# Token attention on one Trainium2 core: where the next input's moments are taken, and which engine normalises it

## The chip, the cores and the metric

The kernel runs on one core of a Trainium2 chip. The metric is the device time of one execution in microseconds (us), given as the median of several runs. The engines are TensorE (PE, with its weight loads shown apart as PEld), VectorE (DVE), ScalarE (ACT), GpSimd (POOL) and SyncE (SP).

## What is computed

The kernel is a stack of four residual blocks, each `x = x + layernorm(f(layernorm(x)))`. The change touches the first one alone, the token attention, on an input of 32 sequences of 256 tokens by 128 features:

```python
def _layernorm(x, axis=-1, eps=1e-05):
    m = jnp.mean(x, axis=axis, keepdims=True)
    v = jnp.var(x, axis=axis, keepdims=True)
    return (x - m) / jnp.sqrt(v + eps)

x = x + _layernorm(_L0_attn_ref(_layernorm(x, axis=-1), ...), axis=-1)
```

`_L0_attn_ref` has 16 heads of 8 features. Its scores are `alpha * tanh(q k / beta)` plus two bilinear terms in tanh bits of the input; then come a causal mask, a softmax over 256 tokens, the values and an output projection.

## The kernel before, in words

**Pipeline.** `token_attention` (from line 482 on) takes one sequence of 256 tokens, two tiles of 128, through four stages. In each step of the pipeline four sequences are in flight: `ahead` (its input is normalised and transposed), `front` (q, k, v and the bilinear left side are projected), `back` (scores, softmax, the first half of the values) and `done` (the rest: last transposes, division, output projection, the norm of the output and the residual). 32 sequences take 35 steps; 30 steps have both `ahead` and `back`, steps 2 to 31.

**Turns.** A step has six turns, 0 to 5. Each turn handles two of the twelve score units (128 x 512) of `back`, the "twins": PE computes raw and bilinear scores (L848, L854) and adds the mask (L858); ACT takes the tanh (L787); DVE sums (L672) and takes the negated row maximum (L682); POOL adds it (L613); ACT takes the exponential one turn later (`EXP = 1`, L804); PE transposes two turns later (`LAG = 2`, L868), and ACT (L748) and DVE (L710) copy the transposes out of PSUM. Every engine runs its own fixed program, in order; semaphores order the engines against each other. PSUM is used as two rings of four banks, one drained by ACT and one by DVE, so PE must wait for an older drain before it fills a bank: the second bilinear unit of a turn needs the bank of an earlier sum.

**What is placed where.** The constants at the head say which turn has which small job: k of `front` is projected in turn 1 and copied by ACT in four activations (L765); `DIVIDE = 3` is the division by the softmax sum (L691, L693 on DVE); `BACK = 4` is the transpose of the result (PE L948, ACT copy `oT` by L748), the output projection (PE L958) and its copy `y` (DVE L726); `OUT = 5` has the moments of `y` on DVE and, on POOL, `yvar` and `yrstd` ahead of the addition of turn 5 and `token_residual` behind it (L456, L459 and L462: subtract the mean, multiply by the inverse deviation, add to x).

**The input's norm, before.** `MOMENTS, SCALE = 1, 3`. At the end of turn 1, behind both maxima, DVE takes the moments of the next input's two tiles (two of L194, a small wait-separating copy at L150, two of L197). At the head of turn 2, ahead of that turn's addition, POOL computes `var` (L183), `rstd` (L187, a power) and `center = -mean * rstd` (L599, L603). At the end of turn 3 ACT computes `xn` with two activations, `Identity` with scale `rstd` and bias `center` (L811). PE transposes `xn` in turn 4 (L900).

The order of one turn on POOL, which matters most here, is:

```python
for i in range(turns):
    if ahead and i == MOMENTS + 1:
        norm.rsqrt(pool, "", ahead)
    ...
    for name in twins(i) if back else []:
        ...  # L613, the addition of the negated maximum
    if done and i == OUT and not done.last:
        token_residual(nc, pool, entry, done)
```

Of the kernel before, what the change touches and what calls it, by code (L numbers as in the profile page):

```python
# [10 lines left out]
ACT = mybir.ActivationFunctionType  # L11
ALU = mybir.AluOpType
AX = mybir.AxisListType

P = 128
# [466 lines left out]
def token_attention(nc, n_seq, x, w, c, behind, entry, following):  # L482
# [10 lines left out]

    VALUES, LATE_VALUES = {5: "yT0"}, {2: "yT1"}
    DIVIDE, BACK, OUT = 3, 4, 5
    MOMENTS, SCALE = 1, 3
    ahead_at = {4: ["xnT"], 5: ["right"]}
    front_at = {0: ["left", "q"], 1: ["k"], DIVIDE: ["v0", "v1"]}

# [28 lines left out]
    with ExitStack() as ctx:  # L528
        def sb(name, shape, dt=F32):
            return ctx.enter_context(nc.sbuf_tensor("t_" + name, shape, dt))  # L530

        def sem(name):
            return ctx.enter_context(nc.semaphore("t_" + name))
# [13 lines left out]
        inv_den = sb("inv_den", [P, TILES * TH])  # L547
        o = sb("o", [P, TILES, D])
        oT = sb("oT", [P, T])
        center = sb("center", [P, TILES])  # L550
        zero = sb("zero", [P, TILES])
        act_banks = [ctx.enter_context(nc.psum_tensor(f"t_act{i}", [P, BANK], F32)) for i in range(RING)]
        dve_banks = [ctx.enter_context(nc.psum_tensor(f"t_dve{i}", [P, BANK], F32)) for i in range(RING)]

# [12 lines left out]
        exped = Count(sem("exped"), in_turns(EXP), [], units[:2 * (turns - EXP)], late(EXP))  # L567
        den = Count(sem("den"), ["o"], [], [], ["o"])
        y, norm, vec, rst, updated = entry.y, entry.norm, entry.vec, entry.rst, entry.updated
        centred = Count(sem("centred"), ["minus", "center"], ["minus", "center"])  # L570
        scaled = Count(sem("scaled"), ["xn0", "xn1"], ["xn0", "xn1"])
        setup_pool, setup_act, setup_dve, setup_pe = (sem("setup_" + e) for e in ("pool", "act", "dve", "pe"))

        lam, scl = w["scalars"][:, 0:1], w["scalars"][:, 1:2]
# [7 lines left out]
        with nc.Block() as block:  # L582
            @block.gpsimd
            def _(pool):
                nc.gpsimd.memset(bilinear[:, :, :, :, :], 0.0).then_inc(setup_pool, 1)


                for u in range(2):
                    nc.gpsimd.memset(v[u][:, :, :, :], 0.0).then_inc(setup_pool, 1)
                nc.gpsimd.memset(zero[:, :], 0.0).then_inc(setup_pool, 1)  # L590
                pool.wait_ge(setup_pool, 4)
                for u in range(2):
                    nc.gpsimd.memset(v[u][:, :, :, TD:TD + 1], 1.0).then_inc(setup_pool, 1)

                def step(ahead, front, back, done):
                    for i in range(turns):
                        if ahead and i == MOMENTS + 1:
                            norm.rsqrt(pool, "", ahead)
                            nc.gpsimd.tensor_tensor(center[:, :], zero[:, :], norm.mv[""][:, :, 0], ALU.subtract)\  # L599
                                .then_inc(centred.sem, 1)  # L600
                            pool.wait_ge(rst.sem, rst.done("rstd", ahead))
                            pool.wait_ge(centred.sem, centred.done("minus", ahead))
                            nc.gpsimd.tensor_tensor(center[:, :], center[:, :], norm.rstd[""][:, :], ALU.mult)\  # L603
                                .then_inc(centred.sem, 1)
                        if done and i == OUT and not done.last:
                            norm.rsqrt(pool, "y", done)
                        for name in twins(i) if back else []:

                            n, gs, t = unit(name)
                            j = units.index(name)  # L610
                            pool.wait_ge(maxed.sem, maxed.done(name, back))
                            p = probs[:, j % SLOTS, :].rearrange("p (h j) -> p h j", h=len(gs))
                            nc.gpsimd.tensor_tensor(  # L613
                                p, p, neg_max[:, j, 0:len(gs)].unsqueeze(2)
                                .broadcast_to((P, len(gs), P * (t + 1))), ALU.add).then_inc(shifted.sem, 1)

                        if done and i == OUT and not done.last:
                            token_residual(nc, pool, entry, done)

                pipeline(pool, n_seq, step, 4, closing=lambda: following.open_pool(pool))  # L620
# [6 lines left out]
            def _(dve):  # L627
# [70 lines left out]
                def step(ahead, front, back, done):  # L698
                    for i in range(turns):
                        if done and i == OUT and not done.last:  # L700

                            wait_apart(nc, dve, c, to_dve.drained.sem, to_dve.drained.done("out", done))
                            norm.post_copied_moments(dve, done, y)
                        if back:
                            summed(i, back)
                        j, seq = lagging(i, LAG, turns, back, done)
                        if seq:
                            job = "pT" + twins(j)[1]
                            to_dve.wait_filled(dve, job, seq)
                            nc.vector.tensor_copy(pT[:, 2 * j + 1, :], to_dve.bank(job, seq)[:, :])\  # L710
                                .then_inc(to_dve.drained.sem, 1)
                        if back:
                            maxima(i, back)
                        if ahead and i == MOMENTS:
                            if not ahead.first:

                                dve.wait_ge(scaled.sem, scaled.done("xn1", ahead.before()))
                            norm.pre_moments(dve, ahead, x)
                        if done and i == DIVIDE:
                            divide(done)  # L720
                        if done and i == BACK:
                            if not done.first:

                                dve.wait_ge(updated.sem, updated.done("x", done.before()))
                            to_dve.wait_filled(dve, "out", done)
                            nc.vector.tensor_copy(y[:, :, :].rearrange("p a d -> p (a d)"),  # L726
                                                  to_dve.bank("out", done)[:, 0:T])\
                                .then_inc(to_dve.drained.sem, 1)
# [8 lines left out]
            def _(act):  # L737
# [39 lines left out]
                def step(ahead, front, back, done):  # L777
                    for i in range(turns):
# [26 lines left out]
                        for jobs, seq in ((ahead_at, ahead), (front_at, front)):  # L805
                            for job in jobs.get(i, []) if seq else []:
                                projected(job, seq)
                        if ahead and i == SCALE:
                            act.wait_ge(centred.sem, centred.done("center", ahead))
                            for t in range(TILES):  # L810
                                nc.scalar.activation(norm.xn[:, t], ahead.tile(x, t), ACT.Identity,  # L811
                                                     scale=norm.rstd[""][:, t:t + 1], bias=center[:, t:t + 1])\
                                    .then_inc(scaled.sem, 1)

                pipeline(act, n_seq, step, 4)

# [1 line left out]
            def _(pe):  # L818
# [7 lines left out]
                                           w["basis"][:, b, :], twT[:, :], start=True, stop=True)  # L826
                ins.then_inc(setup_pe, 1)
                pe.wait_ge(setup_dve, 11)
                pe.wait_ge(setup_pool, 6)

                def rows(n):

# [61 lines left out]
                def project(job, seq):  # L894
                    u, bank = seq.parity, to_act.bank(job, seq)
                    to_act.wait_free(pe, job, seq)
                    if job == "xnT":
                        for t in range(TILES):
                            pe.wait_ge(scaled.sem, scaled.done(f"xn{t}", seq))
                            ins = nc.tensor.transpose(bank[:, t * P:(t + 1) * P], norm.xn[:, t],  # L900
                                                      c["ident"][:, :])
                    elif job == "right":
                        to_act.wait_drained(pe, "xnT", seq)
                        ins = nc.tensor.matmul(bank[:, 0:T], w["bits"][:, :], xnT[u][:, :], start=True, stop=True)
                    elif job in ("q", "k"):
                        ins = nc.tensor.matmul(bank[:, 0:T], w["t" + job][:, :], xnT[u][:, :],
                                               start=True, stop=True)
                    elif job[0] == "v":
                        t = int(job[1])
                        ins = nc.tensor.matmul(bank[:, 0:D], xnT[u][:, t * P:(t + 1) * P], w["tv"][:, :],  # L910
                                               start=True, stop=True)
                    else:
                        to_act.wait_drained(pe, "right", seq)
                        for j in range(2):
                            ins = nc.tensor.matmul(bank[:, j * T:(j + 1) * T],
                                                   bilinear[:, j].rearrange("a n s b -> a (n s b)"),
                                                   bits[u][0:2 * BITS, 0, :], start=True, stop=True)
                    ins.then_inc(to_act.filled.sem, 1)
# [1634 lines left out]
```

## Time and profile before

| what | value |
|---|---|
| runs of the kernel before | 3971.15, 3981.91, 3981.96 us; median 3981.91 us |
| profiled execution | 3975.32 us, its span 3973.5 us |
| engines busy over the span | PE 95%, DVE 73%, ACT 67%, POOL 49% |
| granted TensorE clock, mean | 0.988 |
| token attention | from about 7 us to about 810 us of the span |

The span is what the profiler saw of the program; the execution's own time is 1.8 us longer. Times in timelines are microseconds from the span's start. "Busy" on PE is modelled from a pipeline and is not work at its peak. A bracket such as [0.88 <-PE ...] says how long the engine sat idle before the row and what the profile takes for the cause.

### The profile page before, as it was taken

The numbers are of one execution on the slowest core, as the hardware profiler recorded it, in microseconds if no ns is written. First come the engines' busy times: TensorE is split into PE (matmuls) and PEld (weight loads), VectorE is DVE, ScalarE is ACT, GpSimd is POOL, SyncE is SP. The second block draws the span as 40 slices with busy tenths as digits, with TensorE's granted clock in tenths as the row PEclk, the third lists the DMA queues.
The fourth block names the chain that finished last, engine by engine and source line by source line (L and its number), as shares of the span: only waits on it lengthen the run. The fifth ranks groups of instructions, "written<-read, shape, count | busy, mean of one in ns | idle before, by whom it ended". The sixth has DMA issues, their size and how long they took to land. (4 is left out here: it accounts for less than half of the span.)

```text
span 3973.5 us, 103557 instructions
## 1 busy us (share of the span) xinstructions
PE 3778.9 (95%) x34587; PEld 2912.5 (73%) x34841; DVE 2908.7 (73%) x6982; ACT 2654.1 (67%) x6409; POOL 1950.9 (49%) x1930
## 2 busy tenths in 40 slices
PE   7999999889999999999999999999999999999999
PEld 5767767657777765777776567777777777789998
DVE  6999999878888856888887855555655565656666
ACT  6999999868888833788886356666666666633333
POOL 4666666667777712667675433343334333411111
PEclk9999999989999989999999999999999999999999
DMA  3000000000000010000000100000000000000000
GB/s 107 1 0 0 0 0 0 1 22 21 20 24 20 20 28 20 14 16 13 16 13 19 31 26 1 0 0 0 0 0 0 0 0 0 0 7 9 9 9 9
DMA packets 69052, 47.64 MB, mean 12 GB/s; under 512 B 38361, under 2 KB 57953, under 8 KB 68833
## 3 DMA queue, kind: packets, MB, share of 16 engines
q1 hardware_dynamic: 68960, 46.43, 4.6%
q8 instruction: 56, 0.92, 0.1%
q14 instruction: 36, 0.29, 0.0%
HBM read 12.62 MB, written 4.19 MB: 4 GB/s over the span
## 5 line engine op out<-in xcount | busy, mean ns | idle before, releaser
L1871 ACT ACTIVATE l_probs<-l_act,l_neg_max 128x128 f32<-128x128 f32 (+1 forms) x1024 | 415.5, 425 | 274.0 <-DVE l_neg_max L1820 271.3
L1799 POOL TENSOR_TENSOR l_probs<-l_probs,l_sums 128x512 f32<-128x512 f32 x384 | 391.0, 1039 | 366.9 <-DVE l_sums L1828 366.9
L613 POOL TENSOR_TENSOR t_probs<-t_probs,t_neg_max 128x512 f32<-128x512 f32 x384 | 391.1, 1040 | 247.4 <-DVE t_neg_max L682 247.2
L1820 DVE TENSOR_REDUCE l_neg_max<-l_act 128x2 f32<-128x512 f32 (+1 forms) x384 | 247.0, 685 | 353.4 <-PE l_act L1983 160.7
L2197 ACT ACTIVATE e_hT<-e_act 128x512 f32<-128x512 f32 x256 | 152.7, 597 | 287.0 <-PE e_act L2218 287.0
L672 DVE SCALAR_TENSOR_TENSOR t_probs<-t_tanh_qk,scalars_sb,t_dve 128x512 f32<-128x512 f32 x384 | 269.7, 744 | 72.8 <-ACT t_tanh_qk L787 42.8
L1084 POOL TENSOR_TENSOR w_invQ<-w_lengthsQ,minus_half 128x16 f32<-128x16 f32 x64 | 243.8, 3810 | 87.8 <-DVE w_lengthsQ L1157 87.8
L2230 PEld LDWEIGHTS e_dve<-e_sb,e_hT 128*128 128x128 f32 x2048 | 269.6, 192 | 16.2 <-ACT e_hT L2197 3.0
L1071 POOL TENSOR_TENSOR w_swappedQ<-w_rawQ,w_table 128x512 f32<-128x512 f32 x128 | 162.1, 1288 | 242.9 <-ACT w_rawQ L1269 242.9
L2230 PE MATMUL e_dve<-e_sb,e_hT 128*128 128x128 f32 x2048 | 270.7, 275 | 2.6 <-ACT e_hT L2197 2.6
L2218 PE MATMUL e_act<-e_xnT,e_sb 128*128 128x256 f32 x1024 | 266.7, 383 | 0.0
L787 ACT ACTIVATE t_tanh_qk<-t_act,t_inv_beta 128x512 f32<-128x512 f32 x384 | 244.7, 697 | 29.3 <-PE t_act L848 29.1
L1376 PE MATMUL w_c<-wqkv_sb,w_hT 128*128 128x512 f32 x512 | 255.2, 622 | 6.0 <-ACT w_rawQ L1269 3.7
L848 PE MATMUL t_act<-t_k,t_q 32*128 32x256 f32 (+1 forms) x2048 | 221.1, 343 | 25.9 <-DVE t_probs L672 25.0
L1838 DVE COPY l_pT<-l_dve 128x512 f32<-128x512 f32 x384 | 242.8, 674 | 1.7 <-PE l_dve L1936 1.7
L682 DVE TENSOR_REDUCE t_neg_max<-t_probs 128x2 f32<-128x512 f32 (+1 forms) x384 | 243.9, 678 | 0.0
L1305 ACT ACTIVATE w_probs<-w_a,w_bias,w_invQ 128x128 f32<-128x128 f32 x512 | 185.5, 467 | 82.9 <-DVE w_bias L1186 82.9
L804 ACT ACTIVATE t_probs<-t_probs 128x512 f32<-128x512 f32 x384 | 230.4, 655 | 13.2 <-POOL t_probs L613 13.0
L1071 POOL TENSOR_TENSOR w_swappedK<-w_rawK,w_table 128x512 f32<-128x512 f32 x128 | 223.7, 1766 | 7.3 <-ACT w_rawK L1269 7.3
L1936 PE MATMUL l_dve<-ident_sb,l_probs 128*128 128x128 f32 x1536 | 208.7, 276 | 17.4 <-POOL l_probs L1799 11.9
L854 PE MATMUL t_dve<-t_bits,t_left 32*128 32x256 f32 (+1 forms) x2048 | 221.1, 343 | 0.0
L1921 PE MATMUL l_act<-l_kT,l_qT 64*128 64x128 f32 (+1 forms) x2048 | 219.6, 343 | 0.1
(257 smaller groups left out, 10283.5 us busy)
## 6 DMA issues: line engine op xcount, KB each, us to landing
w_v_mid<-w_v SPq DMA_DIRECT2D x128, 130.0 KB, 2.3
z<-w_z_copy SPq DMA_DIRECT2D x32, 128.0 KB, 2.0
h<-z SPq DMA_DIRECT2D x32, 128.0 KB
out<-x_sb SPq DMA_DIRECT2D x32, 128.0 KB, 1.8
h<-z SPq DMA_DIRECT2D x32, 127.0 KB
wqkv_sb<-L_ffn_wqkv SPq DMA_DIRECT2D x2, 768.0 KB, 6.7
kv_up_sb<-L_attn_w_kv_up SPq DMA_DIRECT2D x1, 1024.0 KB, 9.5
e_sb<-L_ffn_w SPq DMA_DIRECT2D x1, 1024.0 KB, 5.5
```

Of the source, the lines that this page charges most:

```text
L613: nc.gpsimd.tensor_tensor(p, p, neg_max[:, j, 0:len(gs)].unsqueeze(2) .broadcast_to((P, len(gs), P * (t + 1))), ALU.add).then_inc(shifted. ...
L672: nc.vector.scalar_tensor_tensor(probs[:, j % SLOTS, :], tanh_qk[:, j % TANHS, :], alpha, to_dve.bank("bil" + name, back)[:, :], ALU.mult, ...
L682: nc.vector.tensor_reduce(neg_max[:, j, 0:len(gs)], probs[:, j % SLOTS, :].rearrange("p (h j) -> p h j", h=len(gs)), AX.X, ALU.max, negate ...
L787: nc.scalar.activation(tanh_qk[:, j % TANHS, :], to_act.bank("raw" + name, back)[:, :], ACT.Tanh, scale=inv_beta[:, :])\
L1071: nc.gpsimd.tensor_tensor(swapped[kind][:, t, :].rearrange("p (h a d) -> p h a d", a=2, d=HD // 2), raw[kind][:, t, :].rearrange("p (h a d ...
L1084: nc.gpsimd.tensor_tensor(inv[kind][seq.parity][:, :], length[kind][:, :], c["minus_half"][:, 0:TILES * NH], ALU.pow).then_inc(gps.sem, 1)
L1376: ins = nc.tensor.matmul(of[kind].bank(kind, front)[:, t * BANK:(t + 1) * BANK], hT[:, t * P:(t + 1) * P], w["wqkv"][:, layer, at:at + INNER],
L1799: nc.gpsimd.tensor_tensor(p, p, sums[:, at, 0:len(hs)].unsqueeze(2) .broadcast_to((P, len(hs), P * (t + 1))), ALU.mult).then_inc(divided.s ...
L1820: nc.vector.tensor_reduce(neg_max[:, units.index(name), 0:len(hs)], to_act.bank("s" + name, back)[:, :].rearrange("p (h j) -> p h j", h=le ...
L1871: ins = nc.scalar.activation(probs[:, at % SLOTS, s * width:(s + 1) * width], bank[:, s * width:(s + 1) * width], ACT.Exp, bias=neg_max[:, ...
L2218: ins = nc.tensor.matmul(to_act.bank(f"h{e}", back)[:, f * T:(f + 1) * T], w["e1"][:, e, f * P:(f + 1) * P], xnT[back.parity][:, :], start ...
L2230: ins = nc.tensor.matmul(to_dve.bank(job, seq)[:, (e % half) * D:(e % half + 1) * D], hT[:, e % 2, f, t * P:(t + 1) * P], w["e2"][:, e, f, :],
```

## The change

The moments of the next input go from the end of turn 1 to the head of turn 0 on DVE. `var` and `rstd` go from the head of turn 2 to the head of turn 0 on POOL. `center`, with its constant `zero`, is gone. The two activations of ACT in turn 3 are gone: POOL computes `xn` behind its additions of turn 1, over both tiles at once, as a subtraction of the mean and a multiplication by `rstd`, both broadcast over the features. PE waits once for the product instead of once for each tile. The diff, without context that says nothing more:

```diff
-    MOMENTS, SCALE = 1, 3
+    MOMENTS, SCALE = 0, 1
...
-        centred = Count(sem("centred"), ["minus", "center"], ["minus", "center"])
-        scaled = Count(sem("scaled"), ["xn0", "xn1"], ["xn0", "xn1"])
+        scaled = Count(sem("scaled"), ["diff", "xn"], ["diff", "xn"])
...
+                def normalised(ahead):
+
+                    def each(a):
+                        return a.unsqueeze(2).broadcast_to((P, TILES, D))
+
+                    if not ahead.first:
+                        to_act.wait_filled(pool, "xnT", ahead.before())
+                    pool.wait_ge(rst.sem, rst.done("rstd", ahead))
+                    nc.gpsimd.tensor_tensor(norm.xn[:, :, :], ahead.tiles(x), each(norm.mv[""][:, :, 0]),
+                                            ALU.subtract).then_inc(scaled.sem, 1)
+                    pool.wait_ge(scaled.sem, scaled.done("diff", ahead))
+                    nc.gpsimd.tensor_tensor(norm.xn[:, :, :], norm.xn[:, :, :], each(norm.rstd[""][:, :]),
+                                            ALU.mult).then_inc(scaled.sem, 1)
...
                     for i in range(turns):
-                        if ahead and i == MOMENTS + 1:
+                        if ahead and i == MOMENTS:
                             norm.rsqrt(pool, "", ahead)
-                            nc.gpsimd.tensor_tensor(center[:, :], zero[:, :], norm.mv[""][:, :, 0], ALU.subtract)\
-                                .then_inc(centred.sem, 1)
-                            pool.wait_ge(rst.sem, rst.done("rstd", ahead))
-                            pool.wait_ge(centred.sem, centred.done("minus", ahead))
-                            nc.gpsimd.tensor_tensor(center[:, :], center[:, :], norm.rstd[""][:, :], ALU.mult)\
-                                .then_inc(centred.sem, 1)
...
+                        if ahead and i == SCALE:
+                            normalised(ahead)
...
+                        if ahead and i == MOMENTS:
+                            if not ahead.first:
+
+                                dve.wait_ge(scaled.sem, scaled.done("xn", ahead.before()))
+                            norm.pre_moments(dve, ahead, x)
                         if back:
                             summed(i, back)
...
-                        if ahead and i == MOMENTS:
-                            if not ahead.first:
-
-                                dve.wait_ge(scaled.sem, scaled.done("xn1", ahead.before()))
-                            norm.pre_moments(dve, ahead, x)
...
-                        if ahead and i == SCALE:
-                            act.wait_ge(centred.sem, centred.done("center", ahead))
-                            for t in range(TILES):
-                                nc.scalar.activation(norm.xn[:, t], ahead.tile(x, t), ACT.Identity,
-                                                     scale=norm.rstd[""][:, t:t + 1], bias=center[:, t:t + 1])\
-                                    .then_inc(scaled.sem, 1)
...
                     if job == "xnT":
+                        pe.wait_ge(scaled.sem, scaled.done("xn", seq))
                         for t in range(TILES):
-                            pe.wait_ge(scaled.sem, scaled.done(f"xn{t}", seq))
```

## Rows read from the trace of the kernel before

**Rows 1.** Busy time by stretch: us, then PE, PEld, DVE, ACT, POOL, clock, DMA.

```profile
100.00:700.00 600.00, 553.13 (x7733) 421.42 (x7782) 545.55 (x1106) 548.25 (x1159) 407.12 (x529) 1.00 0.00 0
```

**Rows 2.** Timeline of DVE: start, us of the group, engine, line, op, out<-in, count, [idle before].

```profile
410.40 1.27 DVE L682 TENSOR_REDUCE t_neg_max<-t_probs 128x4 f32<-128x512 f32 x2
412.55 1.41 DVE L672 SCALAR_TENSOR_TENSOR t_probs<-t_tanh_qk,scalars_sb,t_dve 128x512 f32<-128x512 f32 x2 [0.88 <-PE t_dve L868]
...
418.14 1.27 DVE L682 TENSOR_REDUCE t_neg_max<-t_probs 128x2 f32<-128x512 f32 x2
419.32 0.48 DVE L194 BATCH_NORM_STATS2 t_stats<-x_sb 128x6 f32 x2
...
420.35 1.41 DVE L672 SCALAR_TENSOR_TENSOR t_probs<-t_tanh_qk,scalars_sb,t_dve 128x512 f32<-128x512 f32 x2 [0.21 <-PE t_act L888]
...
426.94 0.42 DVE L693 TENSOR_TENSOR t_o<-t_dve,t_inv_den 128x256 f32<-128x256 f32 x1
427.61 1.41 DVE L672 SCALAR_TENSOR_TENSOR t_probs<-t_tanh_qk,scalars_sb,t_dve 128x512 f32<-128x512 f32 x2 [0.24 <-ACT t_tanh_qk L787]
```

**Rows 3.** Timeline of ACT in the same step, turns 1, 3 and 4.

```profile
416.94 1.17 ACT L804 ACTIVATE t_probs<-t_probs 128x512 f32<-128x512 f32 x2
417.99 1.57 ACT L765 ACTIVATE t_k<-t_act,places_sb 128x256 f32<-128x256 f32 x4
419.42 1.31 ACT L787 ACTIVATE t_tanh_qk<-t_act,t_inv_beta 128x512 f32<-128x512 f32 x2
...
425.10 0.63 ACT L804 ACTIVATE t_probs<-t_probs 128x512 f32<-128x512 f32 x1 [0.37 <-POOL t_probs L613]
425.63 0.41 ACT L771 COPY t_v<-t_act 128x128 f32<-128x128 f32 x2
425.94 0.88 ACT L811 ACTIVATE t_xn<-x_sb,t_center,t_rstd 128x128 f32 x2
426.72 1.26 ACT L787 ACTIVATE t_tanh_qk<-t_act,t_inv_beta 128x512 f32<-128x512 f32 x2
...
428.32 0.41 ACT L748 COPY t_oT<-t_act 128x256 f32<-128x256 f32 x1
```

**Rows 4.** Timeline of POOL: residual, addition of turn 0, norm, addition of turn 2.

```profile
413.15 0.61 POOL L456 TENSOR_TENSOR t_yn<-t_y,t_ymv 128x256 f32<-128x256 f32 x1
...
415.35 2.04 POOL L613 TENSOR_TENSOR t_probs<-t_probs,t_neg_max 128x512 f32<-128x512 f32 x2
...
420.89 0.20 POOL L183 TENSOR_TENSOR t_var<-t_mv,eps 128x2 f32<-128x2 f32 x1
421.16 0.71 POOL L187 TENSOR_TENSOR t_rstd<-t_var,minus_half 128x2 f32<-128x2 f32 x1
421.84 0.19 POOL L599 TENSOR_TENSOR t_center<-t_zero,t_mv 128x2 f32<-128x2 f32 x1
...
423.03 2.04 POOL L613 TENSOR_TENSOR t_probs<-t_probs,t_neg_max 128x512 f32<-128x512 f32 x2 [0.72 <-DVE t_neg_max L682]
```

**Rows 5.** Timeline of PE in the same step, turn 4.

```profile
425.67 0.38 PE L848 MATMUL t_act<-t_k,t_q 32*128 32x256 f32 x2
...
427.42 0.44 PE L948 MATMUL t_act<-ident_sb,t_o 128*128 128x128 f32 x2 [0.16 <-DVE t_o L693]
...
428.78 0.71 PE L958 MATMUL t_dve<-t_out_sb,t_oT 128*128 128x128 f32 x4 [0.70 <-ACT t_oT L748]
429.42 0.38 PE L848 MATMUL t_act<-t_k,t_q 32*128 32x128 f32 x2
```

**Rows 6.** Timeline of DVE in the next step: turn 5, and the moments again.

```profile
433.64 0.69 DVE L710 COPY t_pT<-t_dve 128x512 f32<-128x512 f32 x1 [0.21 <-PE t_dve L868]
...
443.17 0.48 DVE L194 BATCH_NORM_STATS2 t_stats<-x_sb 128x6 f32 x2
```

**Rows 7.** The residual's line 462: what its engine waited for (us, times).

```profile
  POOL t_yn L459: 6.0, 28
```

**Rows 8.** Timeline of PE near the start, the transpose of the second sequence.

```profile
25.50 0.77 PE L900 MATMUL t_act<-ident_sb,t_xn 128*128 128x128 f32 x2 [1.61 <-ACT t_xn L811]
```

More of the change, by code:

```diff
@@ L549, in token_attention @@
         oT = sb("oT", [P, T])
-        center = sb("center", [P, TILES])
-        zero = sb("zero", [P, TILES])
         act_banks = [ctx.enter_context(nc.psum_tensor(f"t_act{i}", [P, BANK], F32)) for i in range(RING)]
@@ L589, in _ @@
                     nc.gpsimd.memset(v[u][:, :, :, :], 0.0).then_inc(setup_pool, 1)
-                nc.gpsimd.memset(zero[:, :], 0.0).then_inc(setup_pool, 1)
-                pool.wait_ge(setup_pool, 4)
+                pool.wait_ge(setup_pool, 3)
                 for u in range(2):
                     nc.gpsimd.memset(v[u][:, :, :, TD:TD + 1], 1.0).then_inc(setup_pool, 1)
+                def normalised(ahead):
[9 more added lines that the diff above has]
+                                            ALU.mult).then_inc(scaled.sem, 1)
                 def step(ahead, front, back, done):
                     for i in range(turns):
-                        if ahead and i == MOMENTS + 1:
+                        if ahead and i == MOMENTS:
                             norm.rsqrt(pool, "", ahead)
-                            nc.gpsimd.tensor_tensor(center[:, :], zero[:, :], norm.mv[""][:, :, 0], ALU.subtract)\
-                                .then_inc(centred.sem, 1)
-                            pool.wait_ge(rst.sem, rst.done("rstd", ahead))
-                            pool.wait_ge(centred.sem, centred.done("minus", ahead))
-                            nc.gpsimd.tensor_tensor(center[:, :], center[:, :], norm.rstd[""][:, :], ALU.mult)\
-                                .then_inc(centred.sem, 1)
                         if done and i == OUT and not done.last:
@@ L828, in _ @@
                 pe.wait_ge(setup_dve, 11)
-                pe.wait_ge(setup_pool, 6)
+                pe.wait_ge(setup_pool, 5)
                 def rows(n):
```

## The prediction

> **What bounds the kernel now.** I read the busy time by stretch first. In the 600 us of steady token attention PE, DVE and ACT are each busy for 91 to 92 percent and POOL for 68 percent [rows 1]. No engine is the bound alone: the step is a ring of waits among three nearly full engines, and only a place on that ring is worth time. So I read the timeline of each engine over one step. The moments start at 419.32 in one step and at 443.17 in the next [rows 2, 6]: a step takes 23.85 us.
>
> The ring, followed through that step. Turn 1 of ACT is contiguous: exponentials 416.94, four copies of k 417.99, tanh of turn 2 at 419.42 [rows 3]. DVE's sum of turn 2 starts 0.93 us after that tanh, at 420.35; it follows the first of the two tanhs, although the row names an old PE event [rows 2]. So in turn 2 ACT is late, and not DVE. From 420.35 DVE then runs without a gap until the quotient at 426.94, waits 0.24 us for the tanh of turn 4, and sums at 427.61 [rows 2]. On PE the quotient's transpose starts at 427.42, 0.06 us behind DVE; the copy oT on ACT starts at 428.32, behind tanh and another copy; the projection follows at 428.78 and the scores of turn 5 at 429.42 [rows 3, 5]. From there PE is full to the transposes of turn 5, for which DVE's copy at 433.64 waits 0.21 us [rows 6]. POOL is beside the ring, with one tight place: three residual operations from 413.15, and without a gap the addition of turn 0 at 415.35 [rows 4]. Its second half ends at 417.39, and ACT's second exponential of turn 1 starts at about 416.94 + 0.53 = 417.47, with 0.53 taken from 425.10 to 425.63 [rows 3, 4]. The slack there is 0.05 us, given a hand-over of 0.03 us (POOL ends at 423.03 + 2.04 = 425.07, ACT starts at 425.10) [rows 3, 4].
>
> **The change part by part.**
>
> *Moments out of turn 1 on DVE.* They take 420.35 - 419.32 less the idle 0.21, which is 0.82 us [rows 2]. The gain is nothing: the sum of turn 2 waits for ACT's tanh anyhow, so the 0.82 us turn into idle time.
>
> *Moments into the head of turn 0 on DVE.* The cover is the idle 0.88 us before 412.55 [rows 2]. The maxima of turn 5 start at 410.40 and the next operation may start 1.18 us later (419.32 - 418.14 for the same pair), at 411.58; with 0.82 us of moments the sum may start at 412.40, before the 412.55 which ACT sets. Cost nothing, by 0.15 us. Were the cover gone, it would cost up to the whole 0.82 us a step. The new wait for `xn` of the sequence before is met since turn 1 of the step before.
>
> *`var` and `rstd` to the head of turn 0 on POOL.* Before, they stood between 420.89 and 421.84, and the addition of turn 2 was idle for 0.72 us behind them and `center` [rows 4]: free. Now they stand between the residual and the addition of turn 0, where POOL has no idle time. The price by start-to-start distances is 421.84 - 420.89 = 0.95 us [rows 4]. Queued behind them is the addition of turn 0, and ACT's exponential of turn 1 waits for that. The addition ends at 417.39 + 0.95 = 418.34, the second exponential starts at 418.37 in place of 417.47, k at 418.90 in place of 417.99, the tanh of turn 2 at 420.33, the sum of turn 2 at 421.26: +0.91 us (0.95 less the slack, with rounding). The scores of turn 3 follow the first half of that sum, since they need its bank, and DVE is contiguous to the quotient, so all of turns 2 and 3 are 0.91 us later. By spans the two operations would be 0.20 + 0.71 = 0.91 us [rows 4], and the delay 0.87 us.
>
> The rows thus give 0.95 by spacing and 0.91 by spans. The Trainium skill, Perfetto Trace Analysis, GPSIMD Engine Instruction, says that spans on this engine don't compose and that one should go by the distance between starts. By that rule the delay is 0.91 a step, otherwise 0.87; over 28 steps the two differ by about 1 us.
>
> *`center` gone from POOL.* The addition of turn 2 waits for DVE's maximum behind it [rows 4]. Nothing.
>
> *Two products on POOL behind the additions of turn 1.* Of the same shape as L456 [rows 4]: 0.61 us each, with the wait between them some 1.4 us, from 420.89 to about 422.3. The next addition waited for its maximum until 423.03 before, and will until about 423.94. Nothing; PE wants `xn` only in turn 4. The nearest bound from above: all of 1.4 us beyond the 422.23 at which `center` ended is still short of 423.03.
>
> *Two activations gone from ACT in turn 3.* 426.72 - 425.94 = 0.78 us of ACT's order [rows 3]. The tanh of turn 4 can then follow PE's raw scores instead. The last of these end at 425.67 + 0.38 = 426.05 [rows 5]; hand-overs in these rows take 0.03 to 0.06 us, and from PE to ACT I allow 0.11 (an estimate, the upper side), so 426.16 in place of 426.72. The sum of turn 4 can start only when the quotient is done, so DVE gains its idle 0.24 us [rows 2]. PE's path is tighter: the quotient's transpose ends at 427.42 + 0.44 = 427.86, so oT can be copied at 427.97 in place of 428.32 [rows 3, 5]. Gain 0.35 us at the projection and at the scores of turn 5. DVE's 0.24 is no closer limit, since its copy of turn 5 waits 0.21 for PE [rows 6]. What is late next is PE itself. From below the gain is 0.24, from above 0.56 (tanh alone); I take 0.35, the row of the wait that remains.
>
> **The sum.** Per step +0.91 - 0.35 = +0.56 us. The residual precedes turn 0 in 28 steps [rows 7], and all of these have `ahead`: 28 x 0.56 = 15.7 us. In steps 2 and 3 no residual stands ahead and only the gain is left, up to 2 x 0.35 = 0.7 us. At the start PE waits 1.61 us for the second sequence's `xn`, which ACT makes late, behind v [rows 8]; POOL will have it early, and the copy xnT can start when v is copied, about 1.3 us earlier. Together 15.7 - 0.7 - 1.3 = +13.7 us. On the profiled execution's 3975.3 us this is 3989.0 us. That execution is 6.6 us below the median of the runs, 3981.9 us; on the median it is 3995.6 us, +0.34 percent.
>
> **The rivals.**
>
> *POOL does not bite (other side).* The place is the second exponential of turn 1. If POOL's delay were under 0.05 us there, because the power runs while the residual is still being written, or because the residual ends sooner, then only the gain of turn 4 is left: 30 x 0.35 + 1.3 = 11.8 us faster, 3970.1 us on the median. For it: the moments are there by 412.4, 3 us before POOL needs them, and ACT loses 0.78 us of work. Against it: POOL works in order, and 415.35 has no idle time before it. It decides if the delay in turn 1 falls below 0.35 us.
>
> *POOL bites and turn 0 of DVE is not covered.* The margin of 0.15 us is small. If the moments end later than the tanh of turn 0 allows, the sums of turns 0 and 1 and with them PE's scores of turn 2 slip too. At worst 0.82 us more on the ring, 28 x 0.82 = 23 us, so 4018 us; with half of it 4007 us. For it: the tanh is only just later than DVE. Against it: the ring's delay lies behind turn 1, so turn 0 keeps its distances.
>
> *The delay is absorbed in part.* With the gain at its upper 0.56 and the delay at its lower 0.87 the step grows by 0.31 us: 28 x 0.31 - 2.0 = +6.7 us, 3988.6 us. This is the lower end of my own case, not a case apart.
>
> **How the numbers follow.** The forecast has 0.62, the first rival 0.23, the second 0.15. Under about 0.3 percent (12 us) a measurement of this kernel cannot tell from no change. My case runs from 3988 to 3999 us, around 3995.6; by the scatter of the runs, 11 us in three, it ends as slower with 0.45 and as same with 0.17. The first rival lies right on the limit of 0.3 percent: same 0.13, faster 0.10. The second: slower 0.13, same 0.02. That makes faster 0.10, same 0.32, slower 0.58. The range goes down to 3970, the first rival, and up to 4008, half of the second's extra cost.
>
> **What would show it right or wrong.** Right: a step of 24.4 us between two moments; on POOL `var` directly behind L462 and the addition directly behind `rstd`; a new idle time on ACT before its exponentials of turn 1, releaser POOL L613, about 0.4 us twice a step; DVE idle about 1.9 us before the sum of turn 2; that before the sum of turn 0 nearly gone; ACT's tanh of turn 4 waiting for PE. Wrong: a step of 23.5 us, with no wait of ACT on POOL in turn 1; or a step over 24.8 us with DVE contiguous through the head of turn 0.

## The result, and the profile after

The changed kernel takes 3984.87 us in the median of 22 runs, the kernel before 3974.2 us in the median of 22. The ratio is 1.0021, 95% interval [1.0012, 1.003]: slower, by about two thirds of the +0.34 percent that were forecast. The interval lies above 1, so 22 runs of each resolve a difference that the prediction held to be too small to tell from no change. The profiled execution's span is 3984.3 us, 10.8 us more than before; of these, 7.3 us are there by the end of the token attention. One run of a later kernel (norm at the head of turn 1) took 4014.07 us, with a mean granted clock of 0.942 where every other listed run has 0.986 to 0.993; no ratio below contains it.

The busy time of 100 to 700 us of the changed kernel, columns as in [rows 1]:

```profile
100.00:700.00 600.00, 544.99 (x7618) 413.44 (x7664) 533.41 (x1082) 529.36 (x1088) 419.85 (x518) 1.00 0.00 0
```

ACT fell from 548 to 529 us of 600, but PE and DVE fell too, by 8 and 12 us: in the same stretch fewer steps are done. Work was taken from ACT, and the ring became slower.

POOL's timeline of one step of the changed kernel, from the residual on, answers to [rows 4]:

```profile
415.85 0.73 POOL L462 TENSOR_TENSOR x_sb<-x_sb,t_yn 128x256 f32 x1 [0.21 <-POOL t_yn L459]
416.53 0.20 POOL L183 TENSOR_TENSOR t_var<-t_mv,eps 128x2 f32<-128x2 f32 x1
416.81 0.71 POOL L187 TENSOR_TENSOR t_rstd<-t_var,minus_half 128x2 f32<-128x2 f32 x1
417.49 2.04 POOL L617 TENSOR_TENSOR t_probs<-t_probs,t_neg_max 128x512 f32<-128x512 f32 x2
420.07 2.03 POOL L617 TENSOR_TENSOR t_probs<-t_probs,t_neg_max 128x512 f32<-128x512 f32 x2 [0.56 <-DVE t_neg_max L688]
422.07 0.61 POOL L599 TENSOR_TENSOR t_xn<-x_sb,t_mv 128x256 f32<-128x256 f32 x1
422.76 0.61 POOL L602 TENSOR_TENSOR t_xn<-t_xn,t_rstd 128x256 f32<-128x256 f32 x1
425.10 2.04 POOL L617 TENSOR_TENSOR t_probs<-t_probs,t_neg_max 128x512 f32<-128x512 f32 x2 [1.73 <-DVE t_neg_max L688]
```

The norm stands without a gap between the residual and the addition of turn 0, and holds that addition back by 417.49 - 416.53 = 0.96 us. The two products end at 423.4, and POOL then idles 1.73 us: they cost nothing.

ACT's timeline in the same step, turns 1, 3 and 4, answers to [rows 3]:

```profile
418.56 0.63 ACT L810 ACTIVATE t_probs<-t_probs 128x512 f32<-128x512 f32 x1 [0.31 <-POOL t_probs L617]
419.55 0.63 ACT L810 ACTIVATE t_probs<-t_probs 128x512 f32<-128x512 f32 x1 [0.37 <-POOL t_probs L617]
420.09 1.55 ACT L771 ACTIVATE t_k<-t_act,places_sb 128x256 f32<-128x256 f32 x4
421.52 1.28 ACT L793 ACTIVATE t_tanh_qk<-t_act,t_inv_beta 128x512 f32<-128x512 f32 x2
...
428.23 1.26 ACT L793 ACTIVATE t_tanh_qk<-t_act,t_inv_beta 128x512 f32<-128x512 f32 x2
429.38 0.59 ACT L754 COPY t_pT<-t_act 128x512 f32<-128x512 f32 x1
429.97 0.37 ACT L754 COPY t_oT<-t_act 128x256 f32<-128x256 f32 x1
```

Both exponentials of turn 1 now wait for POOL, and k and the tanh of turn 2 are late with them.

DVE's timeline, the answer to [rows 2]:

```profile
411.58 1.27 DVE L688 TENSOR_REDUCE t_neg_max<-t_probs 128x4 f32<-128x512 f32 x2
412.77 0.48 DVE L194 BATCH_NORM_STATS2 t_stats<-x_sb 128x6 f32 x2
...
413.35 0.24 DVE L197 BATCH_NORM_AGGREGATE t_mv<-t_stats 128x2 f32<-128x6 f32 x2
413.70 1.41 DVE L678 SCALAR_TENSOR_TENSOR t_probs<-t_tanh_qk,scalars_sb,t_dve 128x512 f32<-128x512 f32 x2
...
419.32 1.27 DVE L688 TENSOR_REDUCE t_neg_max<-t_probs 128x2 f32<-128x512 f32 x2
422.43 1.41 DVE L678 SCALAR_TENSOR_TENSOR t_probs<-t_tanh_qk,scalars_sb,t_dve 128x512 f32<-128x512 f32 x2 [1.84 <-PE t_act L868]
...
429.02 0.42 DVE L699 TENSOR_TENSOR t_o<-t_dve,t_inv_den 128x256 f32<-128x256 f32 x1
429.36 1.40 DVE L678 SCALAR_TENSOR_TENSOR t_probs<-t_tanh_qk,scalars_sb,t_dve 128x512 f32<-128x512 f32 x2
```

The moments fill the idle time ahead of the sum of turn 0, which starts 413.70 - 411.58 = 2.12 us after the maxima of turn 5; before it was 2.15 [rows 2]. From the maxima of turn 1 to the sum of turn 2 it is 422.43 - 419.32 = 3.11 us; before, 2.21. This is the loss: 0.90 us. The profile lays the 1.84 us of idle time to a PE event; the wait is for ACT's tanh, 421.52 + 0.91, as before the sum came at 419.42 + 0.93 [rows 2, 3]. In turn 4 the sum follows the quotient after 0.34 us, where it took 0.67: DVE waits for ACT no more.

PE's timeline at the end of turn 4, the answer to [rows 5]:

```profile
429.50 0.44 PE L948 MATMUL t_act<-ident_sb,t_o 128*128 128x128 f32 x2 [0.17 <-DVE t_o L699]
...
430.39 0.71 PE L958 MATMUL t_dve<-t_out_sb,t_oT 128*128 128x128 f32 x4 [0.24 <-ACT t_oT L754]
431.04 0.38 PE L848 MATMUL t_act<-t_k,t_q 32*128 32x128 f32 x2
```

The projection comes 0.89 us after the transpose of the quotient; before, 1.36 [rows 5]. This is the gain: 0.47 us in this step. The next `var` on POOL starts at 440.81, so the step is 440.81 - 416.53 = 24.28 us; before, 23.85 [rows 2, 6]. And 0.90 - 0.47 = 0.43.

### The profile page after: what moved, and what is told of

The parts are those of the page before. It is cut to its first block and busy times, and to the rows that moved or that the text cites. A ratio compares the mean times of both kernels' runs of the same rounds, so it can differ in the third digit from the quotient of the medians.

```text
span 3984.3 us, 103435 instructions
## 1 busy us (share of the span) xinstructions
PE 3780.9 (95%) x34587; PEld 2912.8 (73%) x34841; DVE 2906.3 (73%) x6982; ACT 2641.5 (66%) x6345; POOL 1977.2 (50%) x1929
## 5 line engine op out<-in xcount | busy, mean ns | idle before, releaser
L1936 PE MATMUL l_dve<-ident_sb,l_probs 128*128 128x128 f32 x1536 | 208.1, 275 | 17.8 <-POOL l_probs L1799 12.3
L854 PE MATMUL t_dve<-t_bits,t_left 32*128 32x256 f32 (+1 forms) x2048 | 220.2, 343 | 0.0
```

## The experiments

A step below is the distance between the moments of neighbouring sequences in the steady part; it varies by 0.03 us at most within a run. "Norm" stands for `var` and `rstd` on POOL. Ratios are those of the runs, not of the steps.

| kernel | step, us | ratio to before, 95% interval |
|---|---|---|
| before | 23.84 | |
| the change | 24.28 | 1.0021 [1.0012, 1.0030] |
| norm at the head of turn 1 | 23.39 | 0.9952 [0.9936, 0.9968] |
| products alone | 23.40 | 0.9949 [0.9930, 0.9968] |
| moments alone | 23.86 | 1.0002 [0.9993, 1.0011] |
| moments and norm in turn 0, ACT as before | 24.74 | 1.0060 [1.0045, 1.0076] |
| norm behind the addition of turn 0 | 23.39 | 0.9959 [0.9943, 0.9976] |
| a second power in turn 0 | 24.95 | 1.0075 [1.0054, 1.0096] |

**Norm at the head of turn 1.** The changed kernel, with `var` and `rstd` one turn later on POOL:

```diff
-                        if ahead and i == MOMENTS:
+                        if ahead and i == SCALE:
                             norm.rsqrt(pool, "", ahead)
```

> The changed kernel with var and rstd at the head of turn 1 on POOL, ahead of that turn's addition, in place of the head of turn 0. Theory (the power ahead of the addition of turn 0 is what costs): ACT's waits on POOL in turn 1 are gone, the 0.90 us between the sums of turns 1 and 2 go back to 4.1 us, only the gain of turn 4 (0.47 us, as the trace of the changed kernel has it) is left: a step of 23.4 us, about 17 us less than the kernel before (ratio 0.996). Rival (the two products on POOL, or POOL's load as such, cost): the step stays at 24.3 us and the time at that of the changed kernel, ratio 1.002.

It took 3958.68 us in the median of all its runs against 3977.36 us of the kernel before, where the expectation had 17 us less. POOL's timeline of this kernel, from the residual on:

```profile
405.96 0.73 POOL L462 TENSOR_TENSOR x_sb<-x_sb,t_yn 128x256 f32 x1 [0.21 <-POOL t_yn L459]
406.65 2.03 POOL L617 TENSOR_TENSOR t_probs<-t_probs,t_neg_max 128x512 f32<-128x512 f32 x2
408.65 0.19 POOL L183 TENSOR_TENSOR t_var<-t_mv,eps 128x2 f32<-128x2 f32 x1
408.92 0.71 POOL L187 TENSOR_TENSOR t_rstd<-t_var,minus_half 128x2 f32<-128x2 f32 x1
410.19 2.04 POOL L617 TENSOR_TENSOR t_probs<-t_probs,t_neg_max 128x512 f32<-128x512 f32 x2 [0.56 <-DVE t_neg_max L688]
```

The same two operations, one addition later, stand in a gap that ends with 0.56 us still idle. ACT's waits in that kernel, over 600 us of steady steps:

```profile
ACT t_probs L810 <- POOL t_probs L617: 9.5, 26, 0.4
```

Only the old wait of turn 3 is left, once a step; in the changed kernel the same row has 26.2 us in 75 waits, three a step. The place of `var` and `rstd` is what costs, and not the products or POOL's load, which is the same.

**Products alone.** The kernel before, with `center` and ACT's activations replaced by the two products, behind the additions of turn 2; moments and norm stay at their old places:

```diff
-    MOMENTS, SCALE = 1, 3
+    MOMENTS, SCALE = 1, 2
...
-                        if ahead and i == MOMENTS + 1:
+                        if ahead and i == SCALE:
                             norm.rsqrt(pool, "", ahead)
-                            nc.gpsimd.tensor_tensor(center[:, :], zero[:, :], norm.mv[""][:, :, 0], ALU.subtract)\
...
+                        if ahead and i == SCALE:
+                            normalised(ahead)
...
```

> The kernel before with one part of the change: moments stay at the end of turn 1, var and rstd at the head of turn 2, center and the two activations are gone and POOL takes the two products behind the additions of turn 2. Theory: this is the gain alone, 0.47 us a step, so a step of 23.4 us and about 14 us less than before (ratio 0.9965); POOL's addition of turn 3 may start 0.3 us late, which ACT doesn't feel. Rival (ACT's activations were covered, and what looks like a gain in turn 4 is given back by PE or DVE): step 23.85 us, ratio 1.000.

It took 3958.85 us against 3977.36 us: 18.5 us less, where 14 were expected. The profiles differ by 14.8 us at the end of the token attention (the next stage's first statistics, L322, start at 775.6 us in place of 790.4), so the expected size holds there; the rest of the difference is not explained by the steps. Here the products do delay the next addition, as POOL's timeline shows by the missing idle time behind them:

```profile
416.46 0.61 POOL L599 TENSOR_TENSOR t_xn<-x_sb,t_mv 128x256 f32<-128x256 f32 x1
417.15 0.61 POOL L602 TENSOR_TENSOR t_xn<-t_xn,t_rstd 128x256 f32<-128x256 f32 x1
417.72 2.04 POOL L617 TENSOR_TENSOR t_probs<-t_probs,t_neg_max 128x512 f32<-128x512 f32 x2
```

The additions of turn 3 start 3.26 us after those of turn 2 (414.46), where it was 3.10 in the other kernels. The step is the same to 0.01 us: the exponentials of that turn come late enough. So the relief of ACT alone is worth 0.44 us a step. That `center` is gone from POOL as well is no rival: the addition of turn 2 behind it was idle for 0.72 us even with it [rows 4].

**Moments alone.** The kernel before, with one block of DVE moved:

```diff
+                        if ahead and i == 0:
...
+                            norm.pre_moments(dve, ahead, x)
                         if back:
                             summed(i, back)
...
-                        if ahead and i == MOMENTS:
...
-                            norm.pre_moments(dve, ahead, x)
```

> The kernel before with the moments alone moved, to the head of turn 0 on DVE. Theory: 0.82 us of DVE work leave a place where ACT is late by as much and go into an idle time of 0.88 us: step 23.85 us, ratio 1.000 within 0.001. Rival one (turn 0 is not covered): up to 0.8 us a step more, ratio 1.006. Rival two (DVE bounded turn 2): 0.2 us or more a step less, ratio 0.998.

The ratio is 1.0002 and the step 0.01 to 0.02 us longer. DVE's timeline around turn 0 and ahead of turn 2:

```profile
410.68 1.27 DVE L682 TENSOR_REDUCE t_neg_max<-t_probs 128x4 f32<-128x512 f32 x2
411.86 0.48 DVE L194 BATCH_NORM_STATS2 t_stats<-x_sb 128x6 f32 x2
...
412.80 1.40 DVE L672 SCALAR_TENSOR_TENSOR t_probs<-t_tanh_qk,scalars_sb,t_dve 128x512 f32<-128x512 f32 x2
...
420.63 1.40 DVE L672 SCALAR_TENSOR_TENSOR t_probs<-t_tanh_qk,scalars_sb,t_dve 128x512 f32<-128x512 f32 x2 [0.95 <-PE t_act L888]
```

0.82 us of work left turn 1, and 0.74 us of it came back there as idle time, 0.95 us in place of 0.21 us [rows 2]. Nothing was gained and nothing lost; both rivals fall.

**Moments and norm in turn 0, ACT as before.** On top of the moments alone, `var` and `rstd` at the head of turn 0; `center` stays at the head of turn 2:

```diff
-                        if ahead and i == MOMENTS + 1:
+                        if ahead and i == 0:
                             norm.rsqrt(pool, "", ahead)
+                        if ahead and i == MOMENTS + 1:
```

> The kernel before with moments, var and rstd moved to turn 0; center stays at the head of turn 2 and the two activations on ACT in turn 3. Theory: the cost alone, 0.90 us a step in 28 steps, 24.75 us a step and about 25 us more (ratio 1.0063), with ACT waiting twice for POOL in turn 1. Rival (the power runs beside the residual and is hidden): ratio 1.000.

It took 4001.91 us against 3977.36 us: 24.6 us more. The step is 0.90 us longer, and ACT waits twice in turn 1, as its timeline shows:

```profile
404.01 0.63 ACT L805 ACTIVATE t_probs<-t_probs 128x512 f32<-128x512 f32 x1 [0.32 <-POOL t_probs L614]
405.01 0.63 ACT L805 ACTIVATE t_probs<-t_probs 128x512 f32<-128x512 f32 x1 [0.37 <-POOL t_probs L614]
405.55 1.55 ACT L766 ACTIVATE t_k<-t_act,places_sb 128x256 f32<-128x256 f32 x4
```

The parts add up: +0.90 (this kernel) - 0.44 (products alone) = +0.46 against the +0.44 of the whole change.

**Norm behind the addition of turn 0.** The changed kernel, turn kept, order within the turn reversed:

```diff
                     for i in range(turns):
-                        if ahead and i == MOMENTS:
-                            norm.rsqrt(pool, "", ahead)
...
+                        if ahead and i == MOMENTS:
+                            norm.rsqrt(pool, "", ahead)
                         if ahead and i == SCALE:
                             normalised(ahead)
```

> The changed kernel with var and rstd still in turn 0 on POOL, but behind that turn's addition in place of ahead of it. Theory (only the place ahead of the addition costs): the same as with the norm at the head of turn 1, a step of 23.4 us and ratio 0.995 to the kernel before; ACT doesn't wait for POOL in turn 1. Rival (turn 0 as such is too early, through the moments at its head or DVE and POOL beside each other): a step of 24 us or more.

The step is 23.39 us and the median 3959.16 us against 3974.35 us. Turn 0 is no worse a turn than turn 1; only the side of the addition matters.

**A second power.** The changed kernel, with one more operation on POOL ahead of the addition of turn 0:

```diff
+        spare = sb("spare", [P, TILES])
...
                             norm.rsqrt(pool, "", ahead)
+                            nc.gpsimd.tensor_tensor(spare[:, :], norm.var[""][:, :],
+                                                    c["minus_half"][:, 0:TILES], ALU.pow)
```

> The changed kernel with one more power of the same size behind rstd, ahead of the addition of turn 0; its result is used by nobody. Theory (each us ahead of that addition is a us of the step, no slack is left): by the spacing of 0.68 us of the first power the step goes from 24.28 to 24.96 us, 28 x 0.68 = 19 us more than the changed kernel, about 27 us more than the kernel before (ratio 1.0070). Rival (POOL is only just late and another engine limits the step now, as PE or DVE): less than 0.3 us a step, ratio under 1.005.

The step grew from 24.28 to 24.95 us, by 0.67 us. POOL's timeline in this kernel:

```profile
400.28 0.71 POOL L187 TENSOR_TENSOR t_rstd<-t_var,minus_half 128x2 f32<-128x2 f32 x1
400.96 0.70 POOL L610 TENSOR_TENSOR t_spare<-t_var,minus_half 128x2 f32<-128x2 f32 x1
401.63 4.03 POOL L620 TENSOR_TENSOR t_probs<-t_probs,t_neg_max 128x512 f32<-128x512 f32 x4
```

The spacing of the added operation is 401.63 - 400.96 = 0.67 us, and all of it reaches the step. Its additions of turns 0 and 1 now run together as one group of four: POOL itself is without a gap there. The rival falls; no other engine hides any of it.

Three of these kernels are faster than the kernel before and than the change: norm at the head of turn 1, products alone, and norm behind the addition of turn 0, each at about 0.995 of the kernel before. The intervals don't tell the three apart.

## Why the prediction was right or wrong

The path was right, and what was off are two sizes: the gain of turn 4, 0.35 us where 0.44 to 0.47 were measured, and the base on which the sum was put, 7.7 us too high. The parts in turn:

**The ring, and where POOL is tight: right.** POOL's step "between the residual and the addition of turn 0, where POOL has no idle time" is what the trace and two experiments show. The forecast delay was 0.91 us; the trace has 0.90, and the same part alone cost 0.90 a step.

**Spacing against span: right, and the experiment adds to it.** The two operations hold the addition back by 0.96 us from start to start; their spans sum to 0.91. The second power has a span of 0.70 us and cost 0.67, its spacing. This agrees with the rule of the Trainium skill, Perfetto Trace Analysis, GPSIMD Engine Instruction, that one should time by the distance of starts.

**Moments: right.** Removed from turn 1 for nothing, covered in turn 0. The margin is about as small as said, 0.15 us: the moments of the change end at 413.35 + 0.24 = 413.59 and the sum of turn 0 starts at 413.70, 0.11 us later.

**Products on POOL, `center` gone: right.** They cost nothing behind turn 1, and nothing even behind turn 2.

**The gain of turn 4: right in kind, wrong in size.** This is the step of the sum that failed: "oT can be copied at 427.97 in place of 428.32. Gain 0.35 us". It measured 0.47 us in the step shown, and 0.44 us a step by the products alone. Two small terms made it up. The first is the hand-over from PE to ACT, for which one figure, 0.11 us, was allowed everywhere. It is 0.11 us between the raw scores and the tanh, before (PE ends at 430.30 + 0.28 = 430.58, the tanh starts at 430.69) and after (427.74 + 0.38 = 428.12, and 428.23), so the tanh of turn 4 did come 0.11 us behind PE as forecast. Between the transpose and oT it is only 0.03 us (429.50 + 0.44 = 429.94, oT at 429.97). The second is the way from oT to the projection. I kept the 0.46 us of the rows before; it takes 0.42 (429.97 to 430.39). Before, oT started while the profile still showed the copy ahead of it, 427.86 + 0.60 = 428.46 against 428.32, and is shown as 0.41 us long:

```profile
427.86 0.60 ACT L748 COPY t_pT<-t_act 128x512 f32<-128x512 f32 x1
```

After, it starts as that copy ends and is 0.37 us long. Together the two terms are 0.12 us a step. With the gain at 0.47 us the sum is 28 x 0.44 - 2 x 0.47 - 1.3 = 10.1 us in place of 13.7.

That the medians differ by 10.7 us is no proof of this to the last us: the ratio of 1.0021 alone is 8.3 us, with an interval from 4.8 to 11.9. The profiles have 7.3 us at the end of the token attention, and the other 3.5 us of the spans' 10.8 arise behind it, in code that the change does not touch. The agreement of the steps (0.90 - 0.47 against 24.28 - 23.84) is the firm one.

**The base: off, and the larger part of the miss.** The time of 3995.6 us was put on the median of three runs, 3981.9 us; 22 runs have 3974.2 us. The time of the changed kernel was thus given 10.7 us too high, of which 7.7 us are the base, and 3 us the change. The profiled execution's own time, 3975.3 us, was the better base by chance; the choice between the two was not argued.

**The start: right in size, hidden by something else.** The forecast was 1.3 us less. In the trace of the change the second sequence's xnT is copied at 25.07 us in place of 26.30, and the first tanh of scores starts at 28.87 in place of 30.04: 1.2 us. In the total this does not show by itself. The steady part of the change should add 28 x 0.44 = 12.3 us at the end of the token attention, but the first statistics of the next stage (L322) start at 797.7 where they started at 790.4: only 7.3 us later, 5.0 us less than the steady part says. In the kernel with the norm in turn 1 they start at 775.3, and 30 x 0.46 = 13.8 us account for all but 1.3 us of the 15.1. So about 1.3 of the 5.0 us belong to the change, and the rest, 3.7 us, to what the last section tells.

**The rivals.** "POOL does not bite" fell with the first waits; its condition, a delay under 0.35 us in turn 1, came true only in the kernels that move the norm. Its price, 11.8 us faster, was too small: with the gain at 0.45 it is 30 x 0.45 + 1.3 = 14.8 us, and the kernels that have the gain alone are 15.2 to 18.7 us faster in the median. "Turn 0 of DVE is not covered" fell with the moments alone. The chances put 0.58 on slower by over 0.3 percent; with the right size of the gain the likeliest case would have been within 0.3 percent.

## What to carry to other kernels

An engine that is busy two thirds of the time can still have a place without a gap: put a small job on it by reading its timeline around that place, and then put it behind the operation that others wait for, not ahead of it. Here two operations of 0.96 us decided the sign of a change whose other part, 0.8 us of work taken from a full engine, was sound; on the other side of one addition the same code gives 0.995 in place of 1.002. Taking work from a full engine gains only up to the next wait, so size that gain by the hand-overs that remain, from rows, and not by the work removed.

## What the runs showed of the hardware that was not expected

In the first steps PE's score matmuls are slower, and the point at which they become fast moves by 10 us between kernels that differ little. The changed kernel's L854 on PE at the start:

```profile
28.21 0.64 PE L854 MATMUL t_dve<-t_bits,t_left 32*128 32x256 f32 x2
30.90 0.48 PE L854 MATMUL t_dve<-t_bits,t_left 32*128 32x256 f32 x2
31.22 0.38 PE L854 MATMUL t_dve<-t_bits,t_left 32*128 32x256 f32 x2
```

The same line in the kernel with the norm behind the addition of turn 0:

```profile
26.24 0.48 PE L854 MATMUL t_dve<-t_bits,t_left 32*128 32x256 f32 x2
26.56 0.38 PE L854 MATMUL t_dve<-t_bits,t_left 32*128 32x256 f32 x2
```

The same matmuls take 0.64 or 0.38 us. In the kernel before they still take 0.64 us at 35.1 us, and in the kernel with the norm in turn 1 at 33.9 us. The kernels with the norm behind turn 0 and in turn 1 have steady steps of the same 23.39 us, yet the one that is fast from 26 us on reaches the next stage at 771.4 us and the other at 775.3: 3.9 us from the start alone, over half of the 7.3 us that the change makes at that point.

The mean granted clock seems to deny that this is the clock. By the view of busy time, for 20 to 30 us the changed kernel has

```profile
20.00:30.00 10.00, 8.94 (x38) 5.58 (x36) 0.45 (x2) 5.09 (x13) 0.89 (x2) 1.00 1.02 339
```

that is, 1.00 of the 2.4 GHz level, while PE works at the longer durations. But the trace's own list of granted clocks has no entry before 29.0 us in this kernel, 35.8 in the kernel before, 37.5 with the norm in turn 1 and 24.2 with the norm behind turn 0, and the view shows 1.00 where nothing is listed. Each list begins, with the upper level, just where that kernel's matmuls become fast. The kernel with moments and norm in turn 0 shows the rest. Its list begins at 24.3 us, and the clock then falls to the lower level between 27.7 and 38.0 us; line 855 there is line 854 here:

```profile
28.00:37.50 9.50, 9.50 (x66) 5.44 (x61) 4.63 (x8) 5.22 (x11) 2.04 (x2) 0.50 1.04 366
27.30 0.48 PE L855 MATMUL t_dve<-t_bits,t_left 32*128 32x256 f32 x2
28.37 0.64 PE L855 MATMUL t_dve<-t_bits,t_left 32*128 32x256 f32 x2
40.34 0.38 PE L855 MATMUL t_dve<-t_bits,t_left 32*128 32x256 f32 x2
```

With a granted clock of 0.50, the 1.2 GHz level, the group takes 0.64 us, and at 1.00 it takes 0.38, the very durations of the other kernels. So the slow matmuls of the first steps run at the lower level, and 1.00 in that view is a missing record. The Trainium skill, TensorE: Matmul & The Clock Gate, What's actually happening, says that TensorE starts at 1.2 GHz and that the point at which it becomes fast varies from run to run; the durations here agree with the first. Whether the point moves from run to run of one kernel the runs can't tell, since each kernel has one profile, so that one of two kernels became fast earlier may be luck and no effect of its code.

The scatter of some 15 us between runs of one kernel goes with the mean granted clock, where a run's clock is on record. Of the 22 runs of the change, the three with 0.992 or 0.993 took 3971.1 to 3975.4 us, and the five with 0.986 or 0.987 took 3985.4 to 3990.7 us. As nothing is listed for the first steps, that mean speaks of later stretches: in the profile before, all of the lower level that is listed lies behind 793 us, that is, from the end of the token attention on. What this teaches is that a steady step, read from the trace to 0.01 us, is a sharper measure of such a change than the total.
